# One sandwich layer on one core: a new order between the first sum and the routing, and rows of 132 numbers

## The reference

```python
x = x + _layernorm(_L0_attn_ref(_layernorm(x, axis=-1), ...))   # attention and a small "quantum" feed-forward
x = x + _layernorm(_L0_ffn_ref(_layernorm(x, axis=-1), ...))    # 8 experts, one per token

# end of the first block
attn = attn @ Wo + bo
x1 = _layernorm(x + attn, g1, beta1)
h = x1 @ W1 + b1
qm = h @ Wm + bm
qe = jnp.tanh(qm) * jnp.cos(qm * (jnp.pi / 4))
ha = qe @ Wqo + bqo
ff = ha @ W2 + b2
out = _layernorm(x1 + ff, g2, beta2)

# the second block
router_logits = x_flat @ gate_w
router_probs = jax.nn.softmax(router_logits, axis=-1)
expert_idx = jnp.argmax(router_probs, axis=-1)
expert_w = jnp.take_along_axis(router_probs, expert_idx[:, None], axis=1)[:, 0]
for e in range(NUM_EXPERTS):
    h = jax.nn.gelu(x_flat @ w1[e] + b1[e], approximate=False)
    y = h @ w2[e] + b2[e]
    out = out + jnp.where(expert_idx == e, expert_w, 0.0)[:, None] * y
```

## Time and profile before

| | us |
|---|---|
| three runs | 609.52, 611.13, 611.45 (median 611.13) |
| the profiled execution | 610.51, its span 608.7 |
| busy in the span: DVE, PE, ACT, POOL | 416.2, 380.7, 326.3, 278.1 |
| mean granted TensorE clock in it | 0.830 of full speed |

### The profile page before, as it was taken

One profiled execution on the slowest core, in us unless ns is written; L12 is line 12 of the kernel. 1 busy time (PEld: TensorE's weight loads), 2 busy tenths in 40 slices (PEclk: granted clock), 3 DMA queues, 4 the chain that ended last, 5 costly groups with the idle time before them and its releaser, 6 DMA issues.

```text
span 608.7 us, 8343 instructions
## 1 busy us (share of the span) xinstructions
PE 380.7 (63%) x2424; PEld 258.9 (43%) x2424; DVE 416.2 (68%) x877; ACT 326.3 (54%) x570; POOL 278.1 (46%) x397
## 2 busy tenths in 40 slices
PE   0877259777788877878787957400100059999980
PEld 0644137444455444444443337400000048888860
DVE  4895656899999999999993343669670004556671
ACT  1253052799988899898984452434100026655540
POOL 7543031444444444444310222457147714888884
PEclk9989775899988999898888996655555569999996
...
GB/s 203 40 130 5 49 31 88 59 153 141 141 143 141 144 133 138 126 140 139 133 54 1 1 0 1 1 0 1 0 78 104 104 216 201 227 236 230 230 39 0
DMA packets 71176, 60.86 MB, mean 100 GB/s; under 512 B 17667, under 2 KB 62215, under 8 KB 71132
## 3 DMA queue, kind: packets, MB, share of 16 engines
...
## 4 chain that ended last, share of the span: by engine, by line
DVE 40%; PE 26%; issue 19%; POOL 6%; ACT 3%; DMA 3%; ACTq 1%; SPq 1%; POOLq 0%; DVEq 0%
DVE mxs L1519 10%; DVE big L1619 9%; DVE big L1591 8%; PE ps L1359 7%; PE ps L1370 6%; POOL late_s L675 2%; PE ps L1191 2%; DVE gb L1433 1%; PE ps L1204 1%; DVE proj L1735 1%; PE ps L1315 1%; PE ps L1349 1%; DMA bc2q_row<-in_L_attn_bc2q_dram 1%; PE ps L1033 1%; PE ps L1316 1%
## 5 line engine op out<-in xcount | busy, mean ns | idle before, releaser
L1591 DVE SCALAR_TENSOR_TENSOR big<-big,ps 128x1024 f32<-128x1024 f32 x64 | 74.5, 1216 | 13.6 <-ACT big L833 13.5
L1619 DVE SCALAR_TENSOR_TENSOR big<-big,ps 128x1024 f32<-128x1024 f32 x64 | 76.4, 1214 | 7.4 <-PE ps L1191 7.1
L1519 DVE TENSOR_REDUCE mxs<-ps 128x4 f32<-128x1024 f32 x64 | 76.5, 1217 | 1.6 <-PE ps L1063 1.6
L837 ACT ACTIVATE big<-big 128x1024 f32<-128x1024 f32 x64 | 66.1, 1053 | 10.3 <-DVE big L1619 10.1
L1876 DVE TENSOR_SCALAR arena<-ps,x_all 128x128 f32<-128x128 f32 x48 | 14.6, 347 | 81.7 <-PE ps L1379 60.2
L1178 PE MATMUL ps<-proj 128*128 128x256 f16 x256 | 43.7, 303 | 35.4 <-DVE mxs L1519 22.3
L833 ACT ACTIVATE big<-ps 128x1024 f32<-128x1024 f32 x64 | 63.7, 1016 | 2.9 <-PE ps L1178 2.5
L734 POOL DMA_INDIRECT out_dram<-arena,fidx x48 | 48.9, 1019 | 14.6 <-issue 14.6
L650 POOL CAST mtok<-mxs 128x8 bf16<-128x8 f32 x32 | 6.1, 191 | 103.9 <-DVE mxs L1519 103.9
L1191 PE MATMUL ps<-arena 98*128 98x256 bf16 x256 | 43.6, 299 | 7.6 <-DVE big L1591 5.4
L1359 PE MATMUL ps<-arena,big 128*128 128x256 f32 x192 | 47.1, 389 | 1.1 <-ACT arena L964 1.1
...
## 6 DMA issues: line engine op xcount, KB each, us to landing
...
qk_parts<-proj SPq DMA_DIRECT2D x16, 384.0 KB, 2.9
...
```

The source lines that it names most:

```text
L837: nc.scalar.activation(W[par1][:, n, :], W[par1][:, n, :], ACT.Exp).then_inc(p_ready, 1)
L1519: nc.vector.tensor_reduce(mxs[:, b1 % 2, :, 2 * n:2 * n + 2], src, AX_X, ALU.max, negate=True).then_inc(unit_free, 1)
L1591: nc.vector.scalar_tensor_tensor(W[par][:, n, :], W[par][:, n, :], 10.0, f, ALU.add, ALU.mult).then_inc(unit_free, 1)
L1619: nc.vector.scalar_tensor_tensor(W[par][:, n, :], W[par][:, n, :], 0.05, slot_of("log", b, n), ALU.mult, ALU.add).then_inc(unit_free, 1)
```

## The change

It edits stages 3 to 5.

- **Order of the second sum.** PE turns two groups of `qe` ahead at the start of each half, and the turn of the first half's accumulator moves ahead of the first second sum. ACT runs tanh of the first half before its last square, cosine and tanh of the second half after three squares (cosine first), and its turns one group ahead. `weigh` and its semaphores go by half groups. DVE's and POOL's lists of stage 3 are written anew.
- **The norm factor applied early.** `scale_t` multiplies by `T(3)` alone, as soon as `rb` is there; the shift `be2c_bc` is added by a new step `add_shift`, on POOL for groups 0 to 3 and on DVE for 4 to 7; and the outer factor `T(5)` is applied by `add_x`, four instructions per group that also add x. `shift_x` goes.
- **One-hot rows from undivided logits.** The largest of eight logits is the same before and after multiplication by a positive factor per token, so `gates` and `lg` go, and the one-hot rows are made before `sum_x` of the second half. The factor is applied to the differences of the logits just before their exponential.
- **Rows of 132 numbers.** `ROW` becomes C + 4: the new x less the input's mean, the probability factor, the token number, the row's factor `T(7)` and the mean. `scale_x` and `x2_rows` go; two `std_rows` copies write the factor. In the experts ACT makes the normalised rows (`f_xr`, two instructions per tile, three tiles ahead, into two buffers `fxr`), PE's `f_in` reads them, and DVE's last sum takes two instructions, which also add the mean.

```diff
-    ROW = 2 * C + 2
+    ROW = C + 4
...
+        fxr = cut_up(xf, DEPTH * RS * ROW, RS * C, RS, 2)
...
-            nc.gpsimd.tensor_copy(proj[:, :, 2 * C + 1], tok_id[:, :]).then_inc(step["ids"], 1)
+            nc.gpsimd.tensor_copy(srow[:, :, C + 1], tok_id[:, :]).then_inc(step["ids"], 1)
+            nc.gpsimd.tensor_copy(srow[:, :, C + 3], mv_all[:, 0, :]).then_inc(step["ids"], 1)
...
-            def x2_rows(g):
-                pool.wait_ge(step["x2c"], g + 1)
-                nc.gpsimd.tensor_tensor(rows(g, C, 2 * C), rows(g, 0, C), over_c(mv_all[:, 0, g * GT:(g + 1) * GT]), ALU.add).then_inc(step["x2"], 1)
+            def add_shift(g):
+                pool.wait_ge(step["a1"], g + 1)
+                nc.gpsimd.tensor_tensor(t_of(g), t_of(g), be2c_bc[:, :].unsqueeze(1).to_broadcast([P, GT, C]), ALU.add).then_inc(step["ab"], 1)
...
-                act.wait_ge(step["rho"], g // GH + 1)
+                act.wait_ge(step["nm"], g // GH + 1)
                 for i in range(GT):
                     t = g * GT + i
-                    w = nc.scalar.activation(t_of(g)[:, i, :], t_of(g)[:, i, :], ACT.Identity, bias=tl[:, 11, t:t + 1],
-                                             scale=tl[:, 10, t:t + 1])
-                w.then_inc(step["w"], 1)
+                    a1 = nc.scalar.activation(t_of(g)[:, i, :], t_of(g)[:, i, :], ACT.Identity, bias=tl[:, 11, t:t + 1],
+                                              scale=tl[:, 3, t:t + 1])
+                a1.then_inc(step["a1"], 1)
...
+                if g == NG - 1:
+                    tanh(0)
                 square_y(g)
                 if g + 2 < NG:
                     turn(g + 2)
                 if g == GH - 1:
                     take_acc(0)
-            tanh(0)
             cos(0)
             take_acc(1)
             turn_qe(0)
+            turn_qe(1)
             square_z(0)
-            turn_qe(1)
+            turn_qe(2)
             square_z(1)
+            turn_qe(3)
+            square_z(2)
+            cos(1)
             tanh(1)
-            cos(1)
-            for g in range(2, GH):
-                turn_qe(g)
-                square_z(g)
-            turn_qe(GH)
-            for g in range(GH, NG):
-                if g + 1 < NG:
-                    turn_qe(g + 1)
-                square_z(g)
-                scale_t(g - GH)
+            square_z(3)
+            turn_qe(4)
+            turn_qe(5)
+            square_z(4)
+            scale_t(0)
+            turn_qe(6)
+            square_z(5)
+            turn_qe(7)
+            square_z(6)
+            scale_t(1)
+            square_z(7)
+            scale_t(2)
+            scale_t(3)
             for g in range(GH):
                 square_x(g)
             for g in range(GH, NG):
                 scale_t(g)
+            nc.scalar.activation(hT[:, 0:1], mhalf[:, 0:1], ACT.Exp)
...
+            def f_xr(i, j):
+                s = DEPTH * i + j
+                act.wait_ge(f_rows[j], 16 * (i + 1))
+                if exists(*after(i, j, -2)):
+                    act.wait_ge(fs["xT_ps"], s - 1)
+                for t in range(RS):
+                    xr = nc.scalar.activation(fxr[j % 2][:, t, :], frow[j][:, t, 0:C], ACT.Identity, scale=frow[j][:, t, C + 2:C + 3])
+                xr.then_inc(fs["xr"], 1)
...
+                if exists(*after(i, j, 3)):
+                    f_xr(*after(i, j, 3))
...
+            f_xr(0, 0)
+            f_xr(0, 1)
             f_xT(0, 0)
+            f_xr(0, 2)
...
-            turn_qe(0)
-            second_sum(0)
             turn_acc(1)
-            for g in range(1, NG):
-                turn_qe(g)
-                second_sum(g)
+            for h in range(NH):
+                for g in range(GH * h, GH * (h + 1)):
+                    if g % GH == 0:
+                        turn_qe(g)
+                        turn_qe(g + 1)
+                    second_sum(g)
+                    if g % GH and g + 1 < GH * (h + 1):
+                        turn_qe(g + 1)
...
-                pe.wait_ge(f_rows[j], 16 * (i + 1))
+                pe.wait_ge(fs["xr"], s + 1)
...
+                nc.vector.scalar_tensor_tensor(T(11, h), T(3, h), -1.0, mt, ALU.mult, ALU.mult).then_inc(step["nm"], 1)
...
-            def shift_x(g):
+            def add_shift(g):
+                dve.wait_ge(step["a1"], g + 1)
+                nc.vector.tensor_tensor(t_of(g), t_of(g), be2c_bc[:, :].unsqueeze(1).to_broadcast([P, GT, C]), ALU.add).then_inc(step["ab"], 1)
+            def add_x(g):
+                dve.wait_ge(step["ab"], g + 1)
+                dve.wait_ge(step["rc"], g // GH + 1)
                 for i in range(GT):
                     t = g * GT + i
-                    xb = nc.vector.scalar_tensor_tensor(rows(g, C, 2 * C)[:, i, :], be2c_bc[:, :], tl[:, 5, t:t + 1], x_all[:, t, :],
-                                                        ALU.mult, ALU.add)
-                xb.then_inc(step["xb"], 1)
-
-            def add_x(g):
-                dve.wait_ge(step["w"], g + 1)
-                dve.wait_ge(step["xb"], g + 1)
-                nc.vector.tensor_tensor(rows(g, 0, C), t_of(g), rows(g, C, 2 * C), ALU.add).then_inc(step["x2c"], 1)
+                    x2 = nc.vector.scalar_tensor_tensor(srow[:, t, 0:C], u_sb[:, t, :], tl[:, 5, t:t + 1], x_all[:, t, :], ALU.mult, ALU.add)
+                x2.then_inc(step["x2c"], 1)
...
-            def gates(h):
+            def std_rows(h):
                 dve.wait_ge(step["rd"], h + 1)
-                nc.vector.tensor_tensor(lg[:, h * TH:(h + 1) * TH, :], lx[:, 0, h * TH:(h + 1) * TH, :],
-                                        T(7, h).unsqueeze(2).to_broadcast([P, TH, NE]), ALU.mult).then_inc(step["lg"], 1)
-
-            def scale_x(g):
-                dve.wait_ge(step["rd"], g // GH + 1)
-                dve.wait_ge(step["x2"], g + 1)
-                nc.vector.tensor_tensor(rows(g, 0, C), rows(g, 0, C), over_c(tl[:, 7, g * GT:(g + 1) * GT]), ALU.mult).then_inc(step["xr"], 1)
+                nc.vector.tensor_copy(srow[:, h * TH:(h + 1) * TH, C + 2], T(7, h)).then_inc(step["xr"], 1)
...
+            fold(0)
             queries(0)
             var_y(1)
             weigh(0)
             angle(1)
+            fold(1)
             sum_t(0)
             weigh(1)
             sum_t(1)
             weigh(2)
+            sum_t(2)
             queries(1)
-            sum_t(2)
+            var_z(0)
             weigh(3)
             sum_t(3)
-            var_z(0)
-            weigh(GH)
             var_o(0)
-            sum_t(GH)
-            for g in range(GH + 1, NG):
-                shift_x(g - GH - 1)
-                add_x(g - GH - 1)
-                weigh(g)
-                sum_t(g)
-            shift_x(GH - 1)
-            add_x(GH - 1)
+            weigh(4)
+            gate_o(0)
+            sum_t(4)
+            weigh(5)
+            sum_t(5)
+            logits(0)
+            add_x(0)
+            weigh(6)
+            add_x(1)
+            sum_t(6)
             var_z(1)
+            weigh(7)
+            sum_t(7)
+            add_x(2)
+            add_x(3)
+            var_o(1)
+            gate_o(1)
             for g in range(GH):
                 sum_x(g)
             var_x(0)
-            var_o(1)
             for g in range(GH, NG):
-                shift_x(g)
+                add_shift(g)
+            logits(1)
+            for g in range(GH, NG):
                 add_x(g)
-            gates(0)
-            for g in range(GH):
-                scale_x(g)
+            std_rows(0)
...
+            std_rows(1)
+            nc.vector.tensor_tensor(rt[:, 1, :, :], rt[:, 1, :, :], over_e(tl[:, 7, :]), ALU.mult).then_inc(rsem["e"], 1)
...
-                nc.vector.tensor_tensor(fres[j][:, :, :], fwy[par][:, :, :], frow[j][:, :, C:2 * C], ALU.add).then_inc(fs["res"], 1)
+                for t in range(RS):
+                    add = nc.vector.scalar_tensor_tensor(fres[j][:, t, :], frow[j][:, t, 0:C], frow[j][:, t, C + 3:C + 4], fwy[par][:, t, :],
+                                                         ALU.add, ALU.add)
+                add.then_inc(fs["res"], 1)
```

105 lines of the change are left out of this document (56 added, 49 removed).

## The result

The changed kernel takes 590.35 us (median of 4 runs, 586.74 to 592.25), the kernel before in the same session 611.29 (4 runs, 609.52 to 613.47): ratio 0.965, 95% interval 0.959 to 0.971. I had forecast 591.5 us, within 584 to 600, and faster with a chance of 0.96.

A forecast was written before the change was run, and what follows sets the result against it. DVE bounds the attention, waits between engines stages 3 and 4, PE the experts. Terms -12.9 + 0.7 - 11.7 + 1.3 + 3.0 + 0.2 = -19.4 from 610.51 give 591.1 (591.7 on the median's scale), called 591.5 us, range 584 to 600.

The forecast's parts named there:

- block A: The eight second sums, 41.1 us before: one long gap left, ending at 383.5 us, so 28.2 us, -12.9.
- block B: From the second sums' end to the last new x, 28.2 us before: 28.9 us, +0.7, with POOL late.
- Block C: From the last new x to the one-hot rows, 14.4 us before: scaling, sums and root wait leave the path, -11.7.
- Block D: From the one-hot rows to the places, 8.8 us before: moved sums, a copy and a multiplication, +1.3 us.
- Stores: POOL's 32 stores to the sorted rows: row width doesn't show in their 0.975 us each, 0.
- Start of the experts: First row load to first `f_up`: ACT's copy of tile 0 waits behind tile 1's scaling, +3.0 us.
- Pace of the experts: Expert tiles: PE stays the bound at about 3.9 us a tile; only DVE's last sum adds, +0.2 us once.
- rows pacing the experts: Experts: rows take 4 us under load, delay ACT's bias, tiles grow 0.3 us; time 597, chance 0.14.
- quick stores: Stores to the sorted rows: POOL's cost goes by bytes, 31.2 us would be 16; time 576, chance 0.02.
- the order gains nothing: Second sums: `queries(1)` or a root comes later and the stage keeps its 41 us; time 604, chance 0.03.
- the slower one: Experts: row loads from 5.6 us up add 1.1 us a tile, eating the 19.4; 6 us give 615; chance 0.03.
- More blocking: DVE and POOL block each other seven times, up to 1.0 us each against 2.4 held, +4.6; time 596, chance 0.08.

The follow-up runs named there:

- e6: Changed kernel with rows of 258 numbers again, the added columns zero: median 589.0 us for 589.5, stores +0.34 us.
- e9: Changed kernel with four extra PE matmuls, results unused, filling the gap behind second sum 3: first store at 68.89 us, 0.24 sooner.
- e8: Changed kernel with ACT scaling groups 4 to 7 behind its first two squares, DVE summing groups 2 and 3 behind the one-hot rows: -1.74 us to first store.
- e7: Changed kernel with all eight `add_shift` on DVE, none on POOL: -0.56 us to the first store.
- e11: Changed kernel with new DVE, POOL and ACT lists, queries earlier, three filling matmuls, tile 0 copied before tile 1's scaling: 574.7 us.
- e10: Changed kernel with removed norm work put back before the one-hot rows (+9.94 us to first store) and expert rows scaled twice (experts 116.02 us against 115.09).
- e2: Changed kernel with one-hot rows again behind the second half's sums, variance and root: +5.15 us.
- e3: Changed kernel with PE's and ACT's old order of turns and second sums, DVE and POOL as changed: +7.9 us to first store.
- e4: Changed kernel with `scale_t` waiting for the whole factor, outer one included, as before: +4.95 us.
- e5: Changed kernel with `queries(1)` ahead of `sum_t(2)` on DVE: PE's gap falls from 4.07 to 2.83 us, the end comes 0.73 us sooner.

## Why the prediction was right

The total fell 0.2% off, and a part of that is luck. Without the attention, of which I had expected nothing, the stages changed by -19.9 us where I had -19.4, but block A is 2.3 us better than forecast and block B 1.6 worse, with smaller errors either way in the others. By its own terms, against the two profiled executions:

- **Block A: -12.9, measured -15.2** (41.14 to 25.94). The gap of 4.1 was 4.06. Mis-sized was the price of the clock: I took both sums 4 and 5 as slow (4.1 and 3.7), while it came back after 5.7 us (2.8 in e6), and sums 6 and 7 took 2.2 each where I had up to 2.9. My sentence behind it, that POOL's list wins no more than 1 us from a full clock, holds in size (e9: 0 to 0.24 us) and fails in its reason.
- **Block B: +0.7, measured +2.3** (28.2 to 30.5). The ends, 383.1 and 413.6 where I had 383.5 and 412.4, must be read from the first second sum, which came at 357.2 and not at 355.3: 25.9 and 56.4 us behind it where I had 28.2 and 57.1. The chain I wrote down (third and fourth square, 16 `scale_t`, `add_shift`, `logits`, 16 `add_x`) is there link by link, with 6.25 and 4.29 where I had 6.5 and 4.6; e8 shows it as the path by shortening it. And `sum_x(0)` came 42.7 us behind the first second sum for my 42.8: block B is longer mostly because block A is shorter, since the end of the second sums doesn't set the start of that chain. What was wrong is the reason, the sentence "Now POOL is late": POOL idles 2.93, 2.56 and 3.37 us there, each time waiting for DVE, and without `add_shift` on it, but with it on DVE, the stage gains 0.56 us (e7). The two take turns: POOL's square 3 stands behind its root, DVE's `weigh(4)` behind the sum of that square, POOL's square 4 behind `weigh(4)`. e11, which reorders that round among its other edits, gets 13 us.
- **Block C: -11.7, measured -11.8** (14.4 to 2.6). With e10 it splits: 5.15 for the sums and the root's wait (e2), 4.8 for the multiplications (9.94 - 5.15, two lots of 2.49).
- **Block D: +1.3, measured +1.0** (8.72 to 9.71).
- **Stores: 0, measured -0.4.** 0.970 us each for 0.975, and e6's wide rows give back 0.34 of it.
- **Start of the experts: +3.0, measured +3.3.** Right by two errors that cancel: the rows of tile 1 took 4.05 us to land and not 2.5, but were issued 2.05 us behind tile 0's and not 3.13, and the scaling took 0.59 before ACT went on, not 0.8.
- **Pace of the experts: 0, measured 0; the stage +0.2, measured +0.9.** The rows land in 2.2 us (median), the tiles take 3.89 us. ACT waits for rows in 17 tiles, which is half of what I had named as a sign of being wrong; the tiles stay as they were, since PE waits only 1.1 us for ACT's bias. About half of the 0.9 goes with the clock: e2 and e3, whose mean clock in the first 23 us is 0.93 as before (0.92 after), took 114.8 and 114.7 us for 114.3 before. My 0.7 us of slack for ACT fits e10, where 0.60 more costs 0.05 us a tile.

The parts undone one at a time cost 7.9 (e3), 4.95 (e4) and 9.94 (e10), together 22.8 of the 23.7 us that went between the first second sum and the first store. That they nearly add up fits parts that sit one behind the other on one chain; no run undid two of them at once.

Of the rivals, rows pacing the experts falls (2.2 us to land, where I had 2.7 and 0.7 to spare), quick stores fall (e6), "the order gains nothing" falls (e3), and so does the slower one (2.2 us for the 5.6 that it needed). More blocking: it happened much as I had held it, with `add_x(1)` at 2.92 us for 1.14 as the largest (POOL's L689 and L693 beside it), 3.2 us for my 2.4 with L1766 (1.03 for 0.29) and L1771 (0.95 for 0.28), some 3.6 with `add_x(2)` and `add_x(3)` (2.57 for about 2.2). The Trainium skill's rule on the shared port pair (SBUF — State Buffer, "SBUF: two separate sides"), which I had weighed, is borne out by that row and by e5's 1.03 for 0.29. By that rule the root, which reads SBUF too, would block as well, and the measurement says otherwise: in e11 POOL's root starts at 387.32 and runs 2.90 us, and DVE's `add_x` beside it takes its plain 1.14.

The Trainium skill's line for a DMA (DMA: Bandwidth & Descriptors, "Anatomy of one DMA — SWDGE (gpsimd) path") is for DMAs that GpSimd issues; taken for these, which SP issues, it gives an estimate of 0.3 us for the narrower rows. e6 shows 0.7, so the measured step is twice the estimate, and the medians show neither.
